# Two reorderings inside the layer-0 attention of a four-layer transformer kernel on one Trainium2 core

## The reference

```python
def _layer_norm(x, scale, offset):
    mu = jnp.mean(x, axis=-1, keepdims=True)
    var = jnp.var(x, axis=-1, keepdims=True)
    return (x - mu) * jax.lax.rsqrt(var + LN_EPS) * scale + offset

def _cross_attention(q_in, kv_in, wq, bq, wk, bk, wv, bv, wo, bo, bias_k, bias_v):
    qh = (q_in @ wq + bq).reshape(b, q_len, H, K)
    kh = (kv_in @ wk + bk).reshape(b, t, H, K)      # and vh the same way
    kh = jnp.concatenate([kh, jnp.broadcast_to(bias_k, (b, 1, H, K))], axis=1)
    logits = jnp.einsum('bqhk,bthk->bhqt', qh, kh) / scale
    weights = jax.nn.softmax(logits, axis=-1)
    ctx = jnp.einsum('bhqt,bthk->bqhk', weights, vh).reshape(b, q_len, H * K)
    return ctx @ wo + bo

x = res + _cross_attention(_layer_norm(x, ...), xf_1, ...)   # twice
```

## Time and profile before

| what | us |
|---|---|
| median of 3 runs | 2939.87 |
| lowest and highest | 2934.59, 2940.3 |
| the profiled execution, its own time | 2940.3 |
| its span in the trace | 2938.5 |
| PE busy | 2722.6 (93%) |
| DVE busy | 1423.5 (48%) |
| ACT busy | 777.1 (26%) |
| POOL busy | 370.5 (13%) |
| the eight groups of the two attentions of L0 | about 0 to 700 |
| G = 0 | 0 to about 112 |
| G = 4 | about 386 to 480 |

### The profile page before, as it was taken

The page is one execution under the profiler, slowest core; times in us unless marked ns, Lnnn a source line. Parts: engine busy times, 40 slices in busy tenths (PEclk is TensorE's granted clock), DMA queues, the critical chain, the costliest instruction groups (busy, mean ns, idle before and its releaser), DMA issues. The chain is left out here.

```text
span 2938.5 us, 30245 instructions
## 1 busy us (share of the span) xinstructions
PE 2722.6 (93%) x12184; PEld 1935.4 (66%) x12184; DVE 1423.5 (48%) x2252; ACT 777.1 (26%) x1345; POOL 370.5 (13%) x234
## 2 busy tenths in 40 slices
PE   9999999999799999789999999689998789689999
PEld 7778777787588886444454443378887444378887
DVE  6455664556654331345354544364444454464443
ACT  4331243313411112134353525131111222231110
POOL 0000000000310000124343424220000300130000
PEclk9999999999899999899999998799999999899999
DMA  4101111000100002022121211300001001200001
GB/s 181 58 29 45 42 58 58 29 29 1 61 29 20 11 0 115 16 53 54 44 62 39 65 40 46 116 18 29 29 1 61 26 37 43 89 15 29 29 0 58
DMA packets 37824, 129.89 MB, mean 44 GB/s; under 512 B 8757, under 2 KB 8886, under 8 KB 26938
## 3 DMA queue, kind: packets, MB, share of 16 engines
q1 hardware_dynamic: 37690, 128.01, 12.9%
HBM read 82.23 MB, written 8.39 MB: 31 GB/s over the span
## 5 line engine op out<-in xcount | busy, mean ns | idle before, releaser
L1541 DVE TENSOR_REDUCE l_top<-l_slot 128x1 f32<-128x512 f32 x256 | 170.4, 679 | 191.3 <-PE l_slot L1352 190.5
L1491 ACT ACTIVATE l_weighed<-l_across 128x512 f32<-128x512 f32 (+1 forms) x320 | 183.2, 595 | 299.7 <-PE l_across L1374 296.3
L552 PE MATMUL l_wide<-l_key_map,l_norm 128*128 128x260 f32 x1024 | 235.3, 383 | 2.7 <-ACT l_norm L707 2.3
L552 PEld LDWEIGHTS l_wide<-l_key_map,l_norm 128*128 128x128 f32 x1024 | 191.8, 190 | 32.1 <-ACT l_norm L707 2.7
L1374 PE MATMUL l_across<-l_q_stack,l_k_stack 99*128 99x512 f32 (+1 forms) x320 | 187.2, 590 | 12.3 <-ACT l_weighed L1491 9.3
L1222 POOL TENSOR_TENSOR l_paired<-l_weighed 128x2048 f32<-128x2048 f32 x32 | 145.6, 4549 | 397.4 <-ACT l_weighed L1491 336.3
L888 DVE TENSOR_TENSOR x<-l_added,x 128x512 f32<-128x512 f32 x128 | 87.0, 687 | 80.6 <-PE l_added L131 60.6
L1352 PE MATMUL l_slot<-l_k_stack,l_q_stack 97*128 97x512 f32 x256 | 112.4, 440 | 13.7 <-DMA l_k_stack<-l_k_parts 5.9
L1374 PEld LDWEIGHTS l_across<-l_q_stack,l_k_stack 99*128 99x128 f32 (+1 forms) x320 | 59.1, 186 | 97.2 <-issue 61.2
L129 PE MATMUL l_added<-l_value_map_hi,l_probs_T_hi 128*128 128x512 f32 x256 | 112.1, 438 | 6.7 <-DVE x L888 2.4
L2060 ACT ACTIVATE l2m_hidden<-l2m_up,columns 128x512 f32<-128x512 f32 x64 | 44.2, 692 | 270.5 <-PE l2m_up L131 264.4
(11 more groups left out here) (356 smaller groups left out, 5894.6 us busy)
## 6 DMA issues: line engine op xcount, KB each, us to landing
l_k_stack<-l_k_parts SPq DMA_DIRECT2D x192, 72.0 KB, 2.0
l_q_stack<-l_q_parts SPq DMA_DIRECT2D x192, 64.0 KB, 2.0
l_wk<-in_weights SPq DMA_DIRECT2D x10, 1024.0 KB, 4.8
l_wv<-in_weights SPq DMA_DIRECT2D x10, 1024.0 KB, 4.9
l_wo<-in_weights SPq DMA_DIRECT2D x10, 1024.0 KB, 4.8
l_wqT<-in_weights SPq DMA_DIRECT2D x8, 1024.0 KB, 6.9
l0m_raw<-in_weights SPq DMA_DIRECT2D x8, 1024.0 KB, 4.8
l2m_raw<-in_weights SPq DMA_DIRECT2D x8, 1024.0 KB, 6.0
```

Of the source, the lines that this page charges most:

```text
L552: last = pe.matmul(wide[:, j, 0:W], norm[:, k, at:at + P], key_map[:, k, b, :, :].rearrange("p h c -> p (h c)"), start=k == 0, stop=k == K ...
L1491: act.activation(weighed[0:height(c), (CHUNKS * g + c) % RING, j, :], across[0:height(c), use % 2, :], ACT.Exp)\
L1541: dve.tensor_reduce(top[:, t, j:j + 1], slot[:, i % 2, :], AX.X, ALU.max, negate=True).then_inc(s["top_ready"], 1)
```

## The change

It alters two orders, both only in G = 0 and G = 4. No instruction is added or taken away.

```diff
@@ ScalarE, in the loop over G
                 take_bias(G)
                 if first:
-                    take_norm(a, 2, 0)
+                    for k in range(KT):
+                        take_norm(a, 2, k)
                 exps(G, 0)
-                if first:
-                    for k in range(1, KT):
-                        take_norm(a, 2, k)
                 take_turned(G, 0)
@@ VectorE, in the loop over G
                 if first:
                     scale_rows(a, 0)
                     scale_rows(a, 1)
-                take_map(G, range(8))
-                if first:
                     moments(a, 2)
+                    take_map(G, range(4))
                     moments(a, 3)
+                    take_map(G, range(4, 8))
+                else:
+                    take_map(G, range(8))
                 add_learnt(G)
```

## The result

| | before | with the change |
|---|---|---|
| median of 6 runs each, us | 2940.09 | 2957.01 |
| lowest and highest, us | 2934.59, 2943.56 | 2952.03, 2966.42 |
| ratio, 95% interval | | 1.0064 [1.0044, 1.0085] |
| span of the profiled execution, us | 2938.5 | 2951.7 |

The change makes the kernel 0.64% slower by the ratio of the runs (the two medians alone give 0.58%). The forecast was 2958, in a range of 2951 to 2966.

A forecast was written before the change was run, and what follows sets the result against it. The prediction took PE as the bound, other engines costing only when PE waits. It summed 3.2 + 1.7 + 6.0 + 6.0 + 1.2 = 18.1 us onto 2940.3, giving 2958.4, said as 2958, range 2951 to 2966.

The forecast's parts named there:

- DVE edit, G = 0: Value map of G = 0: late low parts make PE start its first key map tile 3.2 us later, at about 34.5.
- DVE edit, G = 4: Value map of G = 4: the low part of tile 4 is done at 400.0, PE wanted it at 398.30, +1.7 us.
- ACT edit, G = 0: Softmax of batch 0 in G = 0: exponential ends 6.58 us later, everything behind moves by +6.0 us.
- ACT edit, G = 4: Softmax of batch 0 in G = 4: the chain around the fourth take stands the same as in G = 0, +6.0 us.
- the clock, both places: Behind the two long PE stalls, G = 0 and G = 4: lower granted clock costs 0.6 us each, 1.2 in all.
- nothing given back between: Behind the late softmax of batch 0: PE and DVE are both full, so no time is given back.
- The banks of the value map: Value map: each bank comes free only when DVE has taken the low part; late ones cost 3.2 and 1.7 us.
- The exponential waits for the last transpose, not for ACT: Softmax of batch 0, G = 0 and 4: exponential stands behind PE's fourth transpose of batch 2, +6.0 us each.
- (b): Rival: ACT's takes are hidden in its idle time or softmax slack; only DVE's 4.9 us remain, 2945; chance 4%.
- (c): Rival: DVE's part is hidden, banks misread or low parts catching up; 13.2 us remain, 2953; chance 8%.
- (a): Rival: the clock costs more, longer falls or falls at short stalls, up to 8.5 instead of 1.2 us, 2965; chance 15%.
- (d): Rival: faster, as work behind L0 meets the low clock's falls differently; 2934 or less; chance 2%.

## Why the prediction was right, step by step

Each term can be read from PE's starts, as the time between two marks less the same before.

| step of the prediction | marks on PE | forecast, us | measured, us |
|---|---|---|---|
| DVE edit, G = 0 | L499 to L513: 17.72, now 20.98 | +3.2 | +3.3 |
| DVE edit, G = 4 | 17.73, now 19.51 | +1.7 | +1.8 |
| ACT edit, G = 0 | L513 to L129: 23.99, now 31.16 | +6.0 | +6.0, and 1.2 left for the clock |
| ACT edit, G = 4 | 23.99, now 30.88 | +6.0 | +6.0, and 0.9 left for the clock |
| the clock, both places | | +1.2 | +2.1 |
| nothing given back between | L129 of G = 0 to L499 of G = 4: 325.28, now 325.36 | 0 | +0.1 |
| sum (of the unrounded differences) | | 18.1 | 19.2 |

The 6.0 in the rows of the ACT edit are DVE's `shift` of batch 1. It began 18.84 us behind L513 before (60.86 - 42.02), and 24.82 in both groups now (69.87 - 45.05 in G = 0). The end of L0 is 18.9 us later and not 19.2, since the value map of G = 0 happened to start 0.2 us earlier.

- *PE is the bound, and an edit costs what it makes PE wait.* Nothing in the eight runs speaks against it. Shown by the DVE order with both moments ahead and by the two takes, whose waits (4.21 and 1.69 us) are those of the arrival times, not of the length of the moved work.
- *The banks of the value map.* Shown by the DVE edit alone. The forecast had PE's first key map tile at 34.5, it started at 34.36.
- *The first `moments` is hidden in G = 4.* The value map of G = 4 stands in one piece of 7.08 us, and the only wait is that at the key map.
- *The exponential waits for the last transpose, not for ACT.* Shown from both sides, by two takes (+1.6 us a place) and by none (0).
- *The two edits add.* Their waits do. In the timed runs 1.0012 and 1.0043 against 1.0064 and 1.0067 say the same within their intervals, which reach 3 to 6 us either way.
- *The clock.* The one term that was mis-sized. I took 0.6 us a place on the ground that part of a slow stretch would pass while PE waits anyway. Six profiled places gave 1.2, 0.9, 1.4, 1.9, 0.9 and 0.8 us, 1.2 in the mean. That is inside the bounds (0 to 3.4), at twice my value. The clock's records in the traces say what was wrong. At each of the six waits of 6.07 us the stretch at the lower level lasted 6.8 us, twice the 3.4 us of the earlier trace rows. Of it 1.2 to 3.4 us passed within the wait. The 3.4 to 5.7 us that were left for PE's work cost half of their length less 0.9 us in all six places (4.2 us cost 1.2, and 5.7 us cost 1.9). These 0.9 us fit the microsecond of slack that the forecast gave PE behind the wait; no run changed that slack by itself. So both grounds for a low value held, and the length of the stretch did not. The short waits brought no fall of their own, as forecast.
- *Rivals.* (b), the takes hidden, and (c), DVE's part hidden, are out by the runs with one edit alone. (a) was right in its direction, but of its 8.5 us only 2.1 were reached. (d), that work behind L0 meets the clock otherwise, is real in kind: it made the profiled execution 5.7 us shorter behind L0. But it is as good as chance and cannot carry a forecast. Behind L0 the ten profiled executions took 2189 to 2199 us for the same work.

The median rose by 16.9 us and the end of L0 by 18.9 in the profile; the interval of the ratio, 13 to 25 us, holds both. What the waits cost was forecast to about a tenth of a microsecond. That the forecast of the total lay within 1 us of the median is partly luck, as the runs of the changed kernel spread over 14 us.

## What to carry to other kernels

On a full engine, a piece of work moved on another engine costs what its bank or its operand then comes late, not what the piece lasts, and both times can be read from the timeline to a tenth of a microsecond. Work that has a gap of its own (here the moments ahead of the learnt sum) gains nothing by being moved out of it. An instruction list that is worked off in order makes a ready exponential wait for the slowest producer of anything put ahead of it, however idle its engine is. To find what can be gained, look for the few waits that the full engine does have: two orders changed in that way gave 0.25%.

## What was not expected of the hardware

- Waits of 2.36, 4.21 and 6.07 us on PE were each followed by work at the lower of the two levels of the clock (3.0 to 3.4 us of it behind the first two, 3.4 to 5.7 us behind the longest), and what that cost did not grow with the wait: about 1.7 us behind the first two, 0.8 to 1.9 us behind the longest. Waits of 1.2 to 1.8 us standing alone were followed by none, and neither was the one wait of 2.78 us, though the shorter one of 2.36 us was in all eight executions that had it. So the length of the wait alone does not say whether the clock falls; what else decides is open. The Trainium skill (TensorE: Matmul & The Clock Gate, "HAM oscillation") tells of a kernel in which the idle gap behind every tile sets the clock back, each time. The trace agrees for the waits of 2.36, 4.21 and 6.07 us, and not for that of 2.78 us.
- The same code with the same waits can meet such a stretch or not. In the last outputs of L0, where PE waits for 1.11 and 0.83 us close together, four of ten profiled executions had a stretch at the lower clock, worth about 1.5 us, and six had not. It happened in kernels whose code there is the same. This is one source of the spread of 5 to 14 us between runs, and the reason why an edit of some microseconds is better read at a mark in the trace than from the total.
